# Two-layer graph kernel on one core: a node block's squares and h go from VectorE to ScalarE, and four more blocks stand beside the first layer

## The reference

```python
edge_index = jnp.stack([src, dst])
h = jnp.maximum(_layernorm(x, axis=-1), 0.0)
x = x + _L0_gnn_ref(h, edge_index, W1, b1, W2, b2)      # two GCN layers
h = jnp.maximum(_layernorm(x, axis=-1), 0.0)
x = x + _L1_gnn_ref(h, edge_attr_64, src, dst, edge_type_32, relation_weight, res_w1, res_w2)

# L0: per layer  h = x @ W ;  agg[dst] += h[src] * dinv[src] * dinv[dst] ;  agg + h * dinv^2 + b ; relu between
# L1: h_proj = einsum('nd,rde->rne', h, relation_weight)
#     att = sum(h_proj[etype, src] * tanh(h_proj[etype, dst] + efeat), -1), softmax over each destination's edges
#     h_nb = segment_sum(h[src] * a)
#     leaky_relu((h + h_nb) @ res_w1.T, 0.01) + leaky_relu(h * h_nb @ res_w2.T, 0.01)
```

## Time and profile before

| | us |
|---|---|
| median of 3 runs | 4308.6 |
| lowest and highest of the 3 | 4300.4, 4341.5 |
| the profiled execution's own time | 4306.9 |
| its span | 4305.2 |
| busy in the span: VectorE | 2725.8 |
| GpSimd | 2838.2 |
| PE | 2019.4 |
| ScalarE | 1416.3 |

### The profile page before, as it was taken

The page is one execution under the profiler, slowest core; times in us unless marked ns, Lnnn a source line. Parts: engine busy times, 40 slices in busy tenths (PEclk is TensorE's granted clock), DMA queues, the critical chain, the costliest instruction groups (busy, mean ns, idle before and its releaser), DMA issues.

```text
span 4305.2 us, 40688 instructions
## 1 busy us (share of the span) xinstructions
PE 2019.4 (47%) x10767; PEld 1571.3 (36%) x10767; DVE 2725.8 (63%) x5251; ACT 1416.3 (33%) x2876; POOL 2838.2 (66%) x4049
## 2 busy tenths in 40 slices
PE   5726989566666312122210000552455566566663
PEld 2214666344444312121110000441344354565553
DVE  9943556588888599999972221475567645444442
ACT  0023658333333222222211000310212122787773
POOL 8887760788888588756317776666666620477787
PEclk9965779555555555555555555755765577666665
DMA  6664656444444355555532222532534342122221
GB/s 242 229 232 137 206 197 214 131 138 137 152 148 130 106 183 172 174 176 164 175 107 59 72 70 62 152 90 58 155 85 124 87 126 87 48 58 58 58 58 29
DMA packets 261686, 547.80 MB, mean 127 GB/s; under 512 B 107792, under 2 KB 119930, under 8 KB 261462
## 3 DMA queue, kind: packets, MB, share of 16 engines
q1 hardware_dynamic: 179702, 445.68, 31.7%
q0 software_dynamic: 81760, 99.52, 9.4%
HBM read 275.18 MB, written 273.83 MB: 128 GB/s over the span
## 4 chain that ended last, share of the span: by engine, by line
POOL 43%; issue 21%; DVE 16%; PE 11%; ACT 5%; DMA 3%; another core or an unknown queue 1%; POOLq 0%; SPq 0%; ACTq 0%; DVEq 0%
POOL arena L1337 16%; POOL result L1332 8%; POOL work L1337 8%; POOL slot_rows L1332 7%; PE banks L1772 3%; POOL pause L1345 3%; PE banks L1764 2%; DMA work<-slot_rows 2%; DVE arena L816 1%; PE banks L1889 1%; DVE arena L824 1%; DVE work L626 1%; DVE arena L620 1%; PE banks L1788 1%
## 5 line engine op out<-in xcount | busy, mean ns | idle before, releaser
L1332 POOL DMA_INDIRECT result<-work,outi x392 | 473.6, 1208 | 307.9 <-DVE work L1039 185.5
L1332 POOL DMA_INDIRECT slot_rows<-work,dsafe x392 | 393.2, 1003 | 283.9 <-POOL pause L1350 143.1
L1337 POOL DMA_INDIRECT arena<-g_by_node_and_edge,m_idx x392 | 432.3, 1103 | 187.4 <-POOL pause L1345 77.6
L1337 POOL DMA_INDIRECT work<-in_x,dsafe x392 | 432.7, 1104 | 147.3 <-issue 57.9
L1337 POOL DMA_INDIRECT arena<-h_by_node_and_edge,m_idx x392 | 410.1, 1046 | 126.4 <-issue 85.0
L1780 PE MATMUL banks<-ident,work 128*128 128x128 f32 x392 | 100.6, 407 | 713.3 <-ACT arena L1489 477.5
L1337 POOL DMA_INDIRECT arena<-input_and_place_by_node,src_i x252 | 308.2, 1223 | 74.6 <-POOL pause L1345 45.4
L1780 PEld LDWEIGHTS banks<-ident,work 128*128 128x128 f32 x392 | 68.8, 213 | 736.9 <-issue 663.6
L1772 PEld LDWEIGHTS banks<-w_sb,work 128*128 128x128 f32 x1568 | 221.4, 225 | 95.0 <-issue 92.7
L1875 PE MATMUL banks<-ident,work 128*128 128x128 f32 x556 | 119.5, 355 | 278.6 <-DMA work<-slot_rows 213.4
L1772 PE MATMUL banks<-w_sb,work 128*128 128x64 f32 x1568 | 236.1, 314 | 2.1 <-ACT work L1478 2.1
(11 more groups left out here) (338 smaller groups left out, 6629.4 us busy)
## 6 DMA issues: line engine op xcount, KB each, us to landing
slot_rows<-work SPq DMA_DIRECT2D x64, 834.0 KB
work<-slot_rows SPq DMA_DIRECT2D x139, 384.0 KB
input_and_place_by_node<-arena SPq DMA_DIRECT2D x49, 528.0 KB
g_by_node_and_edge<-arena SPq DMA_DIRECT2D x49, 512.0 KB
arena<-x_of_destination SPq DMA_DIRECT2D x56, 448.0 KB
work<-g_by_node_and_edge SPq DMA_DIRECT2D x49, 512.0 KB
h_by_node_and_edge<-work SPq DMA_DIRECT2D x49, 512.0 KB
work<-h_by_node_and_edge SPq DMA_DIRECT2D x56, 448.0 KB
```

The source lines that it names most:

```text
L1332: pool.indirect_dma_start(out=table[:, :], out_offset=bass.IndirectOffsetOnAxis(ap=idx, axis=0), in_=of, in_offset=None, bounds_check=boun ...
L1337: pool.indirect_dma_start(out=to, out_offset=None, in_=table[:, :], in_offset=bass.IndirectOffsetOnAxis(ap=idx, axis=0)).then_inc(signal, 16)
```

## The change

`q_square` on ScalarE now squares x1 itself, column by column: 16 activations of 64 elements a partition, each with minus the mean of its column as bias and the sum of its squares written out as accumulator. VectorE makes no centred block and no sum of squares any more. h is made on ScalarE too, as 16 activations relu(x1 * r + (-mean * r)), with r = 1/std as scale; VectorE makes -mean * r (128x16) and signals `Q["scaled"]`. `leaky` reads one operand from PSUM, where the product lies, and the other from the copy; so PE may write the banks again only after it (`Q["lk"]`, `f["lk"]` in place of the copy's signal). `Q_EARLY` goes from 20 to 24. ScalarE and PE take a block's steps behind the edge group's work instead of ahead of it. Four rings of semaphores for gathers become one, `got`.

```diff
-Q_EARLY = 20
+Q_EARLY = 24
...
             def q_centre(b):
                 oq.do(v.tensor_reduce(st[:, 0, :], cols(x1), AX.X, ALU.add))
-                oq.do(ts(st[:, 1, :], st[:, 0, :], 1.0 / D, None, ALU.mult))
-                tt(cols(qxc), cols(x1), wide(st[:, 1, :], CB), ALU.subtract).then_inc(T["centered"], 1)
+                ts(st[:, 1, :], st[:, 0, :], -1.0 / D, None, ALU.mult).then_inc(T["centered"], 1)
 
             def q_variance(b):
                 st = q_stat[:, b % 2]
                 dve.wait_ge(T["square"], NB + b + 1)
-                oq.do(v.tensor_reduce(st[:, 0, :], cols(qsq), AX.X, ALU.add))
+                after(dve, Q["hn"], b - 1)
                 ts(st[:, 2, :], st[:, 0, :], 1.0 / D, EPS, ALU.mult, ALU.add).then_inc(T["var"], 1)
 
             def q_h_rows(b):
                 oq.do(v.reciprocal(st[:, 4, :], st[:, 3, :]))
-                after(dve, q_h[b % 2], 16 * (b // 2))
-                after(dve, Q["hturned"], 2 * (b - 1))
-                stt(out=cols(qh[:, b % 2]), in0=cols(qxc), scalar=0.0, in1=wide(st[:, 4, :], CB),
-                    op0=ALU.max, op1=ALU.mult).then_inc(Q["hn"], 1)
+                tt(st[:, 2, :], st[:, 1, :], st[:, 4, :], ALU.mult).then_inc(Q["scaled"], 1)
...
             def q_result(b):
                 dve.wait_ge(Q["os"], 2 * (b + 1))
-                oq.do(leaky(qlk[:, b % 2], qlk[:, b % 2]))
+                link(leaky_of(qlk[:, b % 2], bank(4, 2), qlk[:, b % 2]), Q["lk"], b + 1)
...
             def q_square(b):                       # ScalarE
+                st = q_stat[:, b % 2]
                 act.wait_ge(T["centered"], NB + b + 1)
-                activation(qsq, qxc, ACT.Square).then_inc(T["square"], 1)
+                for c in range(CB):
+                    ins = activation(cols(qsq)[:, c, :], cols(qx[:, b % QX])[:, c, :], ACT.Square, bias=st[:, 1, c:c + 1],
+                                     accum_out=st[:, 0, c:c + 1])
+                ins.then_inc(T["square"], 1)
+
+            def q_h_rows(b):
+                st = q_stat[:, b % 2]
+                act.wait_ge(Q["scaled"], b + 1)
+                after(act, q_h[b % 2], 16 * (b // 2))
+                after(act, Q["hturned"], 2 * (b - 1))
+                for c in range(CB):
+                    ins = activation(cols(qh[:, b % 2])[:, c, :], cols(qx[:, b % QX])[:, c, :], ACT.Relu,
+                                     bias=st[:, 2, c:c + 1], scale=st[:, 4, c:c + 1])
+                ins.then_inc(Q["hn"], 1)
...
                 if g + 1 < GE:                     # ScalarE, first layer's group g
                     e_mat(g + 1)
                     e_square(g + 1)
-                for k in beside_e(g):
-                    step_q(k)
                 e_turned(g, 0)
                 e_turned(g, 1)
+                for k in beside_e(g):
+                    q_root(k - 1)
                 e_hidden(g, 0)
                 e_hidden(g, 1)
                 for k in beside_e(g):
+                    step_q(k)
+                    if 1 <= k <= NB:
+                        q_h_rows(k - 1)
                     if k < NB:
                         q_square(k)
...
             def q_residual(n):                     # PE
                 pe.wait_ge(Q["ht"], n + 1)
-                after(pe, Q["os"], n - 1)
+                after(pe, Q["lk"], n // 2)
...
             for g in range(GE):                    # PE, first layer's group g
-                for k in beside_e(g):
-                    step_q(k)
                 pe.wait_ge(S["a"], g + 1)
...
                 e_output(g, 0)
                 e_output(g, 1)
+                for k in beside_e(g):
+                    step_q(k)
```

More of the change, by code:

```diff
@@ L255, in build @@
         qx = part(work, Z0 + 2 * BW, [QX, BW])
-        qxc = part(work, Z0 + (2 + QX) * BW, [BW])
         qsq = part(work, Z0 + (3 + QX) * BW, [BW])
@@ L340, in build @@
         t_in, t_out = ring("t_x_loaded", 3), ring("t_rows_stored")
-        Q = sems("q", "turned at h relu u g1 added x1 hn hturned ht o os out")
+        Q = sems("q", "turned at h relu u g1 added x1 hn scaled hturned ht o os lk out")
         q_in, q_g1, q_h, q_out = ring("q_loaded", 3), ring("q_g1_stored"), ring("q_h_stored"), ring("q_out_stored")
-        own_got, own_kept = ring("own_x_here", OWN), ring("own_x_stored", OWN)
+        got, own_kept = ring("rows_gathered", NBR), ring("own_x_stored", OWN)
+        OWN_ALL = [16 * GT * len(range(k, GE, OWN)) if k < OWN else 0 for k in range(NBR)]
+        NEAR_ALL = [OWN_ALL[k] + 16 * GT * len(range(k, GE, NBR)) for k in range(NBR)]
+        SUM2_ALL = [NEAR_ALL[k] + 16 * GT * len(range(k, GE, SUM2)) for k in range(SUM2)]
         placed = sem("places_sent")
-        near_got = ring("near_here", NBR)
         S = sems("e", "centered square var std self mat d1 run place a turned at h relu u g1")
@@ L348, in build @@
         zeroed, counted, sort = sem("slots_zeroed"), sem("relations_counted"), sem("sort_steps")
-        sum2_got = ring("sum2_here", SUM2)
         G = sems("d", "d1 mat run x1 h")
@@ L353, in build @@
         fix = sems("fix", "ve act pe sent")
-        nbr_got = ring("neighbour_here", 3)
         C = sems("perm", "mat hs run hf")
@@ L360, in build @@
         edge_steps = sem("edge_steps")
-        f = sems("f", "mat weighed run share nb two masked summed turned t o os half out")
+        f = sems("f", "mat weighed run share nb two masked summed turned t o os lk half out")
         f_in, f_sent = ring("f_loaded"), ring("f_sent")
@@ L386, in all_landed, with own_here, near_here, sum2_here @@
                 eng.wait_ge(signal, counts[q] if isinstance(counts, list) else counts)
+        def own_here(eng, g):
+            eng.wait_ge(got[g % OWN], 16 * GT * (g // OWN + 1))
+        def near_here(eng, g):
+            eng.wait_ge(got[g % NBR], OWN_ALL[g % NBR] + 16 * GT * (g // NBR + 1))
+        def sum2_here(eng, g):
+            eng.wait_ge(got[g % SUM2], NEAR_ALL[g % SUM2] + 16 * GT * (g // SUM2 + 1))
+        def neighbours_here(eng, s):
+            eng.wait_ge(got[s % 3], SUM2_ALL[s % 3] + 16 * GT * (s // 3 + 1))
         def nodes_done(eng):
@@ L631, in step_q @@
                 if 1 <= k <= NB:
-                    q_variance(k - 1)
                     q_h_rows(k - 1)
@@ L1035, in f_post @@
                 dve.wait_ge(f["os"], 4 * (g + 1))
-                of.do(leaky(flk.rearrange("p k f -> p (k f)"), flk.rearrange("p k f -> p (k f)")))
+                made = flk.rearrange("p k f -> p (k f)")
+                link(leaky_of(made, bank(2, 4)[:, 0:GT * P], made), f["lk"], g + 1)
                 link(tt(cols(fhalf), flk[:, :, 0:D], flk[:, :, D:P], ALU.add), f["half"], g + 1)
@@ L1358, in _ @@
                     t = g * GT + k
-                    gather_slowly(own[:, g % OWN, k * D:(k + 1) * D], x, dsafe[:, t:t + 1], own_got[g % OWN])
+                    gather_slowly(own[:, g % OWN, k * D:(k + 1) * D], x, dsafe[:, t:t + 1], got[g % OWN])
             all_landed(pool, t_out, ROWS_STORED)
             pool.wait_ge(T["flat"], NB)
+            all_landed(pool, got, OWN_ALL)
             gather(last_row[:], node_rows, last_i[:, 0:1], placed)
@@ L1372, in _ @@
                     t = g * GT + k
-                    gather_slowly(near[g % NBR][:, k, :], node_rows, src_i[:, t:t + 1], near_got[g % NBR])
+                    gather_slowly(near[g % NBR][:, k, :], node_rows, src_i[:, t:t + 1], got[g % NBR])
             all_landed(pool, e_a, EDGE_ROWS)
@@ L1497, in q_root @@
             def q_root(b):
+                if not 0 <= b < NB:
+                    return
                 st = q_stat[:, b % 2]
@@ L1965, in f_residual @@
                 pe.wait_ge(f["t"], n + 1)
-                after(pe, f["os"], n - 3)
+                after(pe, f["lk"], g)
                 for k in range(min(4, GT - 4 * c)):
```

20 lines of the change are left out of this document (11 added, 9 removed).

## The result

The changed kernel takes **4566.68 us** (median of four runs, 4561.62 to 4585.31) against 4314.31 us (four runs) of the kernel before on the same chip: a ratio of 1.058, 95% interval 1.053 to 1.063, slower. 4560 was forecast. The profiled execution has a span of 4583.6 us, 278.4 more than before.

The account below looks back on a forecast made before the run. GpSimd's gathers were taken to bound the first layer, VectorE the second stage; after the change ScalarE's queue sets both. 4306.9 + 308 + 12 - 64 - 3 = 4560 us, range 4430 to 4710.

Parts of the forecast that it names:

- The loop of E: First layer's edge groups (stage E): block work ahead of the next group's ScalarE root makes a full turn 38.6 us.
- S: Time of a block's 32 small ScalarE activations (16 h, 16 squares) in a row: 11.2 us, bounds 7.7 and 16.0.
- a(g): End of L705 in the kernel before, the last VectorE operation on edge group g in the first layer.
- intervals of 15 to 16 us: First layer's scans in the profile after: expected this far apart where no block stands beside the group.
- cheap: Rival for ScalarE's small activations: accumulator costs nothing, S 7.7 to 9, total 4390 to 4460 us; 15%.
- dear activations: Rival: accumulator read behind each square without overlap, S 14 to 16, total 4690 to 4793 us; 13%.
- E and the stretch behind it: First layer's edge groups +308 us, then +12 for ScalarE's later broken-segment copy, which delays the second stage.
- D: Second stage (1472 to 2212 us before): ScalarE sets turns of 25.4 us; 674 against 738, so -64 us.
- The last stage: Leaky step reading PSUM and PE's new wait for it were both costed at nothing.
- A lighter VectorE: Rival: first layer stays at its gathers' 22.7 us, second stage falls to that pace, total 4173 us; 4%.
- The clock: Rival: PE at its higher clock in the first layer, that stage +170, total 4420 us; 3%.
- full ring: Sign in the first layer: GpSimd would wait for VectorE or ScalarE with its gather ring full, which it never did.

Follow-up runs that it names:

- e3: Changed kernel with the block's turns, products and copies ahead of the first layer's edge group, block leaky steps reading SBUF; ratio 0.997 to the kernel before.
- e8: Changed kernel with the block's 16 squares behind the next group's root in the first layer; ratio 1.019 to the kernel before.
- e1: Kernel before with only Q_EARLY raised from 20 to 24; ratio 0.987 to the kernel before.
- e4: Changed kernel with the edge group's root ahead of the block's squares on ScalarE in the second stage; ratio 1.034 to the kernel before.
- e5: Kernel before with only the last stage's leaky step reading PSUM banks and PE waiting for it; last stage 582.2 us, ratio 1.003.
- e9: Kernel before with the last stage's leaky step reading the banks in four one-bank instructions, PE waiting for the last; last stage 616.5 us, ratio 1.011.
- e7: Kernel before with 24 early blocks; second-stage blocks' squares and h on ScalarE, group's root ahead of squares, leaky steps from SBUF; 4226.89 us, ratio 0.960.
- e6: Kernel before with only PE's wait for the last stage's leaky step, which still reads SBUF copies; last stage 550.5 us, ratio 0.992.
- e10: Kernel before with the last stage's leaky step reading banks and PE's 28 products also waiting for it; last stage 607.5 us, ratio 0.990, called unclear.
- e2: Changed kernel with the last stage's leaky step and PE's wait as before; last stage 549.3 us, ratio 1.047 to the kernel before.

## Why the prediction was right, point by point

*The loop of E* was right in place and size. Forecast 27.4 + S = 38.6 us a full turn; measured 37.8 (1391.67, 1429.43 and 1467.17 are three scans in a row):

```profile
1391.67 2.16 DVE L705 TENSOR_TENSOR_SCAN arena<-arena 128x960 f32<-128x960 f32 x1
1429.43 2.16 DVE L705 TENSOR_TENSOR_SCAN arena<-arena 128x960 f32<-128x960 f32 x1
1467.17 2.16 DVE L705 TENSOR_TENSOR_SCAN arena<-arena 128x960 f32<-128x960 f32 x1
```

e3 and e8 show that it is this loop: each takes something from between a(g) and the root, and the turn shortens by about as much. One sign that I had named isn't there: intervals of 15 to 16 us around a group without a block. Two intervals share such a group, 30.3 and 22.1 us; their sum of 52.4 is about what the loop gives (38.6 + 15.5 = 54.1).

```profile
1263.26 2.16 DVE L705 TENSOR_TENSOR_SCAN arena<-arena 128x960 f32<-128x960 f32 x1
1293.58 2.16 DVE L705 TENSOR_TENSOR_SCAN arena<-arena 128x960 f32<-128x960 f32 x1
1315.70 2.16 DVE L705 TENSOR_TENSOR_SCAN arena<-arena 128x960 f32<-128x960 f32 x1
```

*S, ScalarE's 32 activations*: forecast 11.2, measured 10.6 (5.3 for 16 h, 5.3 for 16 squares: 1438.80 to 1444.11 to 1449.41). The h ones are 0.33 apart, 0.03 above my value; the squares are 0.331 apart, not 0.40. So the sum is close partly because two errors have opposite signs, and the rivals of cheap (7.7 to 9) and dear activations (14 to 16) both fall. The accumulator read is a row of its own of 189 ns, as in my upper bound, but most of it overlaps: the next square starts 0.09 us after the read does. One-pointer rows without an accumulator are 0.24 apart, so the accumulator goes with another 0.09. From the figures of the Trainium skill (ScalarE: Activation LUTs, What ACT_TABLE_LOAD costs) I estimate 0.33 for two pointers at 64 columns, and the rows agree.

*E and the stretch behind it*: forecast +308 and +12 = +320, measured +270.9 and +28.9 = +299.8. The 0.8 us a turn explain 17 of the 20 (21 turns). That +12 came out as +28.9 is a matter of where the scans stand in the turn: VectorE now waits for the root behind the scan, so the last a(g) is 26.6 us behind the last scan (1709.5, the last L679 at 1729.6, and 6.5 to the end) instead of 6.4. I had left that 20 in the first term. The sum isn't touched by it.

*D*: forecast -64, measured -69.6; turns of 24.7 us (25.4 forecast). e1 shows that 45.7 of it is the four blocks; e4 that another 83 us of VectorE's saving were locked up behind the root.

*The last stage* is the term that was wrong: "nothing", measured +44.9 in the profile (594.6 against 549.7) and +32 in e5 alone. The tail behind its last scan is 13.3 us shorter (69.2 against 82.5), which I hadn't forecast and no run explains: it is 79.0 in e5 and 83.6 in e9. I had weighed how long the instruction takes and whether PE's wait binds; both were judged rightly and neither is what costs. All seven kernels whose leaky step reads the banks there took 574 to 630 us, and all five without took 549 to 551. The other terms: the stretch ahead of E +21.9 (within its variation between runs), from D's last scan to the last stage -5.3, of which the step less behind D's last scan, forecast at -3, is 2.9 (38.3 us to the next stage's first scan against 41.2). Sum 270.9 + 28.9 - 69.6 - 5.3 + 44.9 - 13.3 + 21.9 = 278.4, the whole difference of the two spans.

So the forecast's 253 us, which the medians hit (252), were partly luck: E and D came out at 230 where 256 was forecast, and the last stage made up for it.

*The rivals.* A lighter VectorE did not win, for the reason given; e7 shows under what order it does, within 1% of the 4173 that this rival was given (0.960 of 4307 is 4135), though it is another kernel, with the old blocks beside E. The clock stayed (0.54 and 0.53). GpSimd didn't wait with a full ring in E, as I had said it would: it ran through its gathers, with one wait of 11.5 us for the indices that ScalarE casts (L1592), and then waited 340 us in one piece for the stage's end.

```profile
POOL fix_row L1349 <- DMA yer_input_of_destination<-arena: 340.0, 1, 340.0
```

*What stays open*: why, when VectorE reads the banks, 1 to 8 of the last stage's 27 turns take 25 to 36 us (no turn of the other five kernels is over 22.5), with PE and ScalarE standing for up to 16 us. It is not the wait (e6), not the span over several banks (e9), not the overlap with PE's products (e10), and not the length of ScalarE's program (e2 has it, and no stalls). In one such stall of the changed kernel (ScalarE idle from 4013.0 to 4026.9) the trace has the semaphore behind PE's 28 products, recorded as over by 4010.5, at 4024.8, and the one behind its transposes at 4026.9; so PE's results come late, and ScalarE waits rightly. But PE is not alone in it. ScalarE's own last activation before that stall (L1723) is recorded as over at 4013.0, its semaphore comes at 4016.3, and VectorE's scan, which waits for it, starts at 4016.47. In all seven kernels that read the banks, some scans start 1 to 6 us behind the last such row of ScalarE; in the other five always within 0.6. So whatever it is holds more than one engine's results; what it is I can't tell. Whether the block's leaky step, 49 times beside E and D, does the same is not settled: D took 585.5 us with it (e4) and 579.3 without (e7), where the blocks' steps in D are otherwise nearly the same.

## What to carry to other kernels

Moving work to an idle engine isn't priced by that engine's share of busy time, but by what stands behind the work in its queue: here one root of 0.2 us stood behind 10.6 us of small activations, and both other engines waited for it in turn. Before accepting such a move, list what the engine does between the last thing it is given and the next thing that others need from it, and put the handover first; and make it only where the relieved engine is the bound (here D, not E). So done, and with four blocks moved, it was worth 4% instead of costing 6%. The gain ends where the next engine's pace begins, here GpSimd's gathers. And compare stage by stage: a stage of 550 us that grows by 30 is lost in the spread of whole times.

## What the runs showed of the hardware that I had not expected

- A small activation with an accumulator output shows two rows, 335 ns and 189 ns, and such activations in a row are 0.331 us apart, the same as ones with two pointers and no accumulator (0.332).
- A VectorE step that reads one operand from PSUM banks instead of SBUF takes the same time (1217 ns against 1219 at 1024 columns from two banks, 2025 against 2036 at 1792 from four), and yet in the last stage such a step goes with irregular stalls of up to 16 us on other engines: 56 to 104 us of "remote" waits ahead of ScalarE's copy in e5, e9 and e10, against 1.7 in e6.
- PE's granted share of the clock in the last stage was 0.62 with the stalls (changed kernel) and 0.66 without (e7).
